# Attention over batches: the sum of two units in sixteen formed by TensorE with the identity, units handed on in the order 1, 2, 0, 3, product with v six steps behind

## What is computed

```python
# B = 8 batches, 32 heads of width d = 8, HW = 256 positions
xr = x.reshape(B, C, HW).transpose(0, 2, 1).reshape(B, HW, 32, d).transpose(0, 2, 1, 3)
q, k, v = split(einsum('brnd,ed->brne', xr, w_qkv) + b_qkv, 3)
attn = einsum('brnd,brmd->brnm', q, k)
attn = softmax(attn, axis=0)              # over the 8 batches, not over positions
out = einsum('brnm,brmd->brnd', attn, v)
```

## Time and profile before

| | |
|---|---|
| median of three runs | 654.94 us (652.09 to 654.96) |
| the profiled execution | 652.48 us |
| its span, first to last instruction | 650.7 us |
| TensorE busy (matmul / weight load) | 563.1 us (87%) / 359.0 us (55%) |
| VectorE busy | 476.3 us (73%) |
| ScalarE busy | 322.2 us (50%) |
| GpSimd busy | 385.1 us (59%) |
| mean granted TensorE clock | 0.926 of 2.4 GHz |

### The profile page before, as it was taken

The page is one execution under the profiler, slowest core; times in us unless marked ns, Lnnn a source line. Parts: engine busy times, 40 slices in busy tenths (PEclk is TensorE's granted clock), DMA queues, the critical chain, the costliest instruction groups (busy, mean ns, idle before and its releaser), DMA issues.

```text
span 650.7 us, 13039 instructions
## 1 busy us (share of the span) xinstructions
PE 563.1 (87%) x4540; PEld 359.0 (55%) x4541; DVE 476.3 (73%) x845; ACT 322.2 (50%) x687; POOL 385.1 (59%) x240
## 2 busy tenths in 40 slices
PE   3899667999999999999999996689973999999944
PEld 1555346655555555555555553679862565655633
DVE  5547865999999999999999995584866334333325
ACT  2533572677676767677676764232232333333310
POOL 2000371999999999999999997140005566666420
PEclk9998795899999999999999999699955999999985
DMA  6111066133233323333233200000032222222239
GB/s 207 55 47 33 2 224 257 74 105 115 85 90 104 100 85 89 101 101 95 81 97 103 58 1 3 1 1 1 2 122 46 71 87 90 83 82 90 65 106 323
DMA packets 34693, 56.58 MB, mean 87 GB/s; under 512 B 8693, under 2 KB 23438, under 8 KB 34382
## 3 DMA queue, kind: packets, MB, share of 16 engines
q1 hardware_dynamic: 30462, 45.26, 22.3%
q0 software_dynamic: 3744, 10.39, 5.2%
q10 hardware_dynamic: 432, 0.20, 0.1%
HBM read 38.43 MB, written 17.40 MB: 86 GB/s over the span
## 4 chain that ended last, share of the span: by engine, by line
POOL 40%; PE 36%; issue 9%; DVE 8%; DMA 2%; ACT 2%; SPq 1%; POOLq 1%; another core or an unknown queue 0%; DVEq 0%
POOL e_ring L371 39%; PE ps L1336 11%; PE ps L1352 5%; PE ps L1290 2%; PE ps L1092 2%; PE ps L1268 2%; PE ps L1281 2%; PE ps L1122 2%; PE ps L1081 2%; DVE stats L652 1%; PE ps L1228 1%; PE ps L1328 1%; PE ps L1344 1%; SPq L349 1%; PE ps L1068 1%
## 5 line engine op out<-in xcount | busy, mean ns | idle before, releaser
L371 POOL TENSOR_TENSOR e_ring<-e_ring,x_hat 128x1024 f32<-128x1024 f32 x128 | 272.7, 2134 | 35.8 <-ACT x_hat L545 23.6
L535 ACT ACTIVATE e_ring<-ps 128x1024 f32<-128x1024 f32 x128 | 131.1, 1024 | 94.8 <-PE ps L1175 94.8
L792 DVE TENSOR_REDUCE m_bf<-ps 128x128 bf16<-128x1024 f32 x128 | 157.0, 1227 | 10.4 <-PE ps L1166 10.4
L799 DVE TENSOR_REDUCE x_hat<-e_ring 128x128 f32<-128x1024 f32 x128 | 156.4, 1222 | 2.3 <-ACT e_ring L535 2.1
L1166 PE MATMUL ps<-q_stack,k_stack 72*128 72x128 bf16 x1024 | 139.0, 319 | 9.4 <-DMA k_stack<-qk_parts 9.4
L1166 PEld LDWEIGHTS ps<-q_stack,k_stack 72*128 72x128 bf16 x1024 | 103.9, 133 | 35.9 <-issue 35.9
L1175 PE MATMUL ps<-m_bf,ident_neg 128*128 128x512 bf16 x256 | 80.5, 397 | 13.4 <-DVE m_bf L792 5.8
L1189 PE MATMUL ps<-e_ring,v_slot 128*32 128x128 f32 x2048 | 85.4, 283 | 3.6 <-POOL e_ring L371 3.6
L1189 PEld LDWEIGHTS ps<-e_ring,v_slot 128*32 128x32 f32 x2048 | 49.8, 108 | 57.5 <-issue 52.6
L1336 PE MATMUL ps<-w_sb,e_ring 128*128 x156 | 75.4, 607 | 1.2 <-issue 1.2
L406 POOL DMA_INDIRECT pair_rows<-scratch,slot_y x39 | 38.5, 986 | 41.9 <-DVE scratch L1026 28.4
(11 more groups left out here) (150 smaller groups left out, 685.1 us busy)
## 6 DMA issues: line engine op xcount, KB each, us to landing
q_stack<-qk_parts SPq DMA_DIRECT2D x32, 288.0 KB
k_stack<-qk_parts SPq DMA_DIRECT2D x96, 96.0 KB
w_sb<-in_w13T_dram SPq DMA_DIRECT2D x16, 256.0 KB, 6.7
qk_parts<-scratch SPq DMA_DIRECT2D x2, 1536.0 KB, 19.1
qk_parts<-e_ring SPq DMA_DIRECT2D x2, 1152.0 KB, 5.5
x_res<-in_x_dram SPq DMA_DIRECT2D x8, 256.0 KB, 3.9
w_sb<-in_w2T_dram SPq DMA_DIRECT2D x8, 256.0 KB, 6.7
token_rows<-work SPq DMA_DIRECT2D x4, 512.0 KB, 3.0
```

The costliest lines, as they stand in the source:

```text
L371: nc.gpsimd.tensor_tensor(ev, ev, view(x_hat, CH + (u % RS) * P, [[0, BQ], [1, P], [0, 2]]), ALU.mult).then_inc(norm_done, 1)
L535: nc.scalar.activation(e_ring[:, u % ER, :], score_banks(v), ACT.Exp).then_inc(exp_done, 1)
L792: nc.vector.tensor_reduce(m_bf[:, u % 2], by_position(score_banks(v).rearrange("p a c -> p (a c)")), AXY, ALU.max).then_inc(max_done, 1)
L799: nc.vector.tensor_reduce(s_sum[:, u % 2], by_position(e_ring[:, u % ER, :]), AXY, ALU.add).then_inc(sum_done, 1)
```

## The change

The sums of units 0 and 8 of each group (`BY_PE`) are taken from VectorE. TensorE forms them with 8 matmuls each, the f32 identity as weights and the exponentials of one batch as the 128 columns, accumulated in 128 columns of PSUM bank 7. The eight matmuls are spread over three steps (`SUM_PARTS`: batches 0 to 2, 3 to 5, 6 and 7), two, three and four steps behind the unit's scores, between subtract and product. ScalarE's logarithm reads these two sums from bank 7.

Units are handed from the logarithm on in the order 1, 2, 0, 3, ... and 9, 10, 8, 11, ... (`ORDER`). Logarithm and inverse run three steps behind instead of two, the product six instead of five (`LAG`), and with it evacuate, transposes and add_heads move one step. `s_sum` becomes a ring of four, and `s_ln` moves to columns behind `s_inv`. New waits: the adds wait for the exponentials, for the logarithm of the sum that was in the bank before, and (unit 8) for add_heads; the transposes wait for the logarithm of unit 0.

```diff
-    LAG = 5
+    LAG = 6
+    ORDER = (1, 2, 0, 3, 4, 5, 6, 7, 9, 10, 8, 11, 12, 13, 14, 15)
+    BY_PE = (0, 8)
+    SUM_PARTS = ((0, 1, 2), (3, 4, 5), (6, 7))
+    RSUM = 4
...
             def weights(k, p):
                 pool.wait_ge(r_done, k + 1)
                 ev = e_ring[:, ORDER[p] % ER, :]
...
             def exponentials(U, v, u):
                 act.wait_ge(sub_done, U + 1)
                 if later_than(U, ER):
-                    act.wait_ge(pv_done, U - ER + 1)
+                    act.wait_ge(pv_done, position(U - ER) + 1)
...
+            def logarithm(k):
+                U = unit(k)
+                if U % UPG in BY_PE:
+                    act.wait_ge(pe_sums, sums_by_pe(U))
+                    total_of = ps[:, 7, 0:P]
+                else:
+                    act.wait_ge(sum_done, sums_by_dve(U))
+                    total_of = s_sum[:, U % RSUM]
+                nc.scalar.activation(s_ln[:, k % 2], total_of, ACT.Ln).then_inc(ln_done, 1)
...
-                if has(2):
-                    logarithm(U - 2, (u - 2) % UPG)
-                    inverse(U - 2, (u - 2) % UPG)
+                if has(3):
+                    logarithm(U - 3)
+                    inverse(U - 3)
...
-            def total(U, u):
+            def total(U):
                 dve.wait_ge(exp_done, U + 1)
-                if later_than(U, 2):
-                    dve.wait_ge(ln_done, U - 1)
+                if U >= RSUM and (U - RSUM) % UPG not in BY_PE:
+                    dve.wait_ge(ln_done, position(U - RSUM) + 1)
...
-                if has(1):
-                    total(U - 1, (u - 1) % UPG)
-                if u == LAG + 2 and has(LAG + 3):
+                if has(1) and (U - 1) % UPG not in BY_PE:
+                    total(U - 1)
+                if u == LAG + 3 and has(LAG + 4):
                     add_heads(g, g)
...
+            def add_batches(U, part):
+
+                batches = SUM_PARTS[part]
+                if part == 0:
+                    pe.wait_ge(exp_done, U + 1)
+                    if U % UPG == BY_PE[1] and U >= UPG:
+                        pe.wait_ge(x2_added, U // UPG)
+                    if U >= UPG // 2:
+                        pe.wait_ge(ln_done, position(U - UPG // 2) + 1)
+                for b in batches:
+                    last = nc.tensor.matmul(ps[:, 7, 0:P], ident[:], view(e_ring, (U % ER) * UW + (b // 2) * (2 * P) + b % 2, [[2, P]]),
+                                            start=(b == 0), stop=(b == B - 1), skip_group_check=True)
+                if part == len(SUM_PARTS) - 1:
+                    last.then_inc(pe_sums, 1)
...
                 if has(1):
                     subtract(U - 1, v - 1, (u - 1) % UPG)
+                for part in range(len(SUM_PARTS)):
+                    if has(2 + part) and (U - 2 - part) % UPG in BY_PE:
+                        add_batches(U - 2 - part, part)
                 if has(LAG):
-                    product(U - LAG, (u - LAG) % UPG, g)
+                    product(U - LAG, g)
                 if u == LAG + 1 and has(LAG + 2):
+                    pe.wait_ge(ln_done, position(g * UPG + BY_PE[0]) + 1)
                     transpose_heads(g)
```

More of the change, by code:

```diff
@@ L129, in conv_stack_kernel @@
                  for buf in (e_ring[:, 2:8, :].rearrange("p a b -> p (a b)"), scratch[:, :])]
-        s_sum = x_hat[:, 0, 0:2 * P].rearrange("p (s n) -> p s n", s=2)
-        s_ln = x_hat[:, 0, 2 * P:4 * P].rearrange("p (s n) -> p s n", s=2)
+        s_sum = x_hat[:, 0, 0:RSUM * P].rearrange("p (s n) -> p s n", s=RSUM)
+        s_ln = x_hat[:, 0, CH + RS * P:CH + (RS + 2) * P].rearrange("p (s n) -> p s n", s=2)
         s_inv = x_hat[:, 0, CH:CH + RS * P].rearrange("p (s n) -> p s n", s=RS)
@@ L206, in conv_stack_kernel @@
         stack_in = [sem(f"stack_in{i}") for i in range(HPG)]
+        pe_sums = sem("pe_sums")
         scores_done, max_done, sub_done, exp_done, sum_done, ln_done = (
@@ L248, in attention_steps, with unit, position, sums_by_pe @@
                 step(UNITS + u, UNITS + u, u, NG, lambda k: k > u)
+        def unit(k):
+            return k // UPG * UPG + ORDER[k % UPG]
+        def position(U):
+            return U // UPG * UPG + ORDER.index(U % UPG)
+        def sums_by_pe(U):
+            return U // UPG * len(BY_PE) + sum(b <= U % UPG for b in BY_PE)
+        def sums_by_dve(U):
+            return U + 1 - sums_by_pe(U)
         def score_banks(v):
@@ L366, in _, with weights @@
                                         parts[s // 2][:, s % 2, 1, c * CH:(c + 1) * CH], ALU.subtract).then_inc(part3, 1)
[L368 to L371, removed]
+            def weights(k, p):
+                pool.wait_ge(r_done, k + 1)
+                ev = e_ring[:, ORDER[p] % ER, :]
+                nc.gpsimd.tensor_tensor(ev, ev, view(x_hat, CH + (p % RS) * P, [[0, BQ], [1, P], [0, 2]]), ALU.mult
                                         ).then_inc(norm_done, 1)
             with pool.Fori(0, NG) as g:
-                for u in range(UPG):
-                    weights(g * UPG + u, u)
+                for p in range(UPG):
+                    weights(g * UPG + p, p)
             for b in range(B):
@@ L535, in exponentials, with inverse @@
                 nc.scalar.activation(e_ring[:, u % ER, :], score_banks(v), ACT.Exp).then_inc(exp_done, 1)
[L537 to L545, removed]
+            def logarithm(k):
[7 more added lines that the diff above has]
+                nc.scalar.activation(s_ln[:, k % 2], total_of, ACT.Ln).then_inc(ln_done, 1)
+            def inverse(k):
+                act.wait_ge(ln_done, k + 1)
+                if k >= RS:
+                    act.wait_ge(norm_done, k - RS + 1)
+                nc.scalar.activation(s_inv[:, k % RS], s_ln[:, k % 2], ACT.Exp, scale=-1.0).then_inc(r_done, 1)
             def evacuate(g):
@@ L793, in maximum @@
                                         ).then_inc(max_done, 1)
-            def total(U, u):
+            def total(U):
                 dve.wait_ge(exp_done, U + 1)
-                if later_than(U, 2):
-                    dve.wait_ge(ln_done, U - 1)
-                nc.vector.tensor_reduce(s_sum[:, u % 2], by_position(e_ring[:, u % ER, :]), AXY, ALU.add).then_inc(sum_done, 1)
+                if U >= RSUM and (U - RSUM) % UPG not in BY_PE:
+                    dve.wait_ge(ln_done, position(U - RSUM) + 1)
+                nc.vector.tensor_reduce(s_sum[:, U % RSUM], by_position(e_ring[:, U % ER, :]), AXY, ALU.add).then_inc(sum_done, 1)
             def add_heads(g, group):
@@ L1178, in subtract, with product @@
                 last.then_inc(sub_done, 1)
-            def product(U, u, g):
+            def add_batches(U, part):
[11 more added lines that the diff above has]
+                    last.then_inc(pe_sums, 1)
+            def product(k, g):
+                p, u = k % UPG, unit(k) % UPG
                 i, mh, nh = u // 4, (u // 2) % 2, u % 2
-                if u % 4 == 0:
-                    pe.wait_ge(v_slot_ready[i], g + 1 if u < UPG - LAG else g)
-                if u == 0 and later_than(U, 1):
+                if p % 4 == 0:
+                    pe.wait_ge(v_slot_ready[i], g + 1 if p < UPG - LAG else g)
+                if p == 0 and k >= 1:
                     pe.wait_ge(acc_out, g)
-                pe.wait_ge(norm_done, U + 1)
+                pe.wait_ge(norm_done, k + 1)
                 for b in range(B):
@@ L1191, in product @@
                                             view(e_ring, (u % ER) * UW + (b // 2) * (2 * P) + b % 2, [[2, P]]),
-                                            start=(u == 0 and b < 4), stop=(u == UPG - 1), skip_group_check=True)
+                                            start=(p == 0 and b < 4), stop=(p == UPG - 1), skip_group_check=True)
                 last.then_inc(pv_done, 1)
```

## The result

The changed kernel takes 663.37 us (median, 660.05 to 664.27); before, with the runs taken beside it, 653.71. The ratio is 1.014, 95% interval 1.0094 to 1.0186. The forecast was 662.7. The profiled execution took 663.47 us with a span of 661.7 us, 11.0 more than before by either.

The account below looks back on a forecast made before the run. VectorE set the pace before; afterwards TensorE's 36.05 us floor plus 1.3 of waits gives 37.35 a group. Groups 5.1, first group 1.8 and end 2.1 sum to +9.0 on 653.7: 662.7 us, range 643 to 671.

Parts of the forecast that it names:

- TensorE's price of the adds: Attention, TensorE: 0.2225 us per f32 identity matmul, 3.56 us a group for sixteen, raising TensorE's floor to 36.05 us.
- The step of 2.00: Attention, TensorE running late: scores, subtraction and product take 0.83 + 0.57 + 0.60 = 2.00 us a step.
- rival C: Attention: a late TensorE step takes 1.85 us, not 2.00; period 35.1, total 644.6 us; chance 0.13.
- VectorE's saving is lost: Attention, steps 2 to 4: TensorE never waits, VectorE idles, and the time taken off VectorE is spent as idleness.
- the walk: Start times followed through a group's 16 attention steps using links from the trace; returned 36.7 us before, 37.35 after.
- Rival A: Attention: the adds fit in and VectorE stays the bound; 18 us saved before losses, total 639.5 us; chance 0.08.
- Rival B: Attention: TensorE's floor without waits sets a 36.05 us period; total 652.3 us, hardly a change; chance 0.15.
- Rivals D and E: D: adds cost more, 0.32 us a matmul, over 675 us, chance 0.08; E: change doesn't do what it says, 0.02.
- Two of the signs given for being right: Attention: VectorE idle 2.5 to 3 us a group before maxima, released by scores; no subtraction wait in steps with adds.
- The period: Attention, one group of 16 units: 36.05 us TensorE floor plus 1.3 of waits, 37.35 us, 0.64 slower.
- The end: End of attention, last exponential to last product: 8.0 us instead of 5.92, so +2.1 us.
- The first group: Start of attention: TensorE at half clock until 117.3 us, first adds at twice the price, 1.8 us more.

Follow-up runs that it names:

- the handing on alone: The change without its adds (VectorE keeps all sixteen totals, later order of handing on stays) against the kernel before: 659.0 us against 655.28, ratio 1.0067.
- one unit: The change with only unit 8 summed by TensorE in f32, unit 0 back on VectorE, against the kernel before: 658.21 us, ratio 1.0085.

## Why the prediction was right, point by point

**TensorE's price of the adds** held: 0.2225 us a matmul was forecast; blocks of 3, 3, 2 made steps of 2.68 and 2.46 where 2.67 and 2.45 were written down, halving gave 0.22 and doubling 0.226 each. The step of 2.00 held in every late step (2.00 to 2.01), so rival C is out: from the first of eight scores to the subtraction it is 0.84 us, 0.105 each. The Trainium skill (TensorE: Matmul & The Clock Gate, Back-to-back issue gap) gives about 81 ns for pairs of load and matmul of 128 columns; these rows don't bear that out.

**VectorE's saving is lost** held in kind. In the first half of the group hardly any of the total's 1.13 us is used: steps 2 to 4 are as long with as without it, and up to step 10 the difference is 0.13. In the second half more is used than the walk had, because the addition of heads stands there. Rival A would have had 639.5 and is out. The Trainium skill (Perfetto Trace Analysis, Identifying the Most-Contended Engine) judges TensorE's room by the busy share of its weight loads, beside the share of peak FLOPs. The trace doesn't bear that share out here: it was 57% before, and yet the group had only 0.66 us of room left behind the adds, and the order of steps took more than that. Rival B (36.05, no waits) is out too: the group is 37.70. Rivals D and E did not occur.

Two of the signs given for being right did not show. VectorE's gaps are 2.1 us a group, not 2.5 to 3, and they lie ahead of the totals, released by exponentials, not ahead of the maxima: the maximum runs as soon as its scores are there, while the exponential that the next total needs stands behind a subtraction that is late in TensorE's queue. And the subtraction does wait in two steps with adds, 0.29 in step 2 and 0.18 in step 10; the walk itself had 0.26 in step 2 and a wait in step 10, so that sign did not agree with the walk.

**The period** was forecast at 37.35 and measured at 37.70: 0.99 a group instead of 0.64. The walked starts of the scores agree with the trace within 0.15 us up to step 10 (23.3 against 23.2); step 10 then takes 3.11 against 2.9. The term that was most too small is that step: its two waits are 0.35 together where I had 0.22, and from the adds, which had to wait, to the product it is 0.85 instead of 0.77. The other 0.14 are some 0.01 a step on TensorE.

**The end** held: +2.1 forecast, 8.00 - 5.92 = 2.08 measured, 2.07 with the handing on alone.

**The first group** is the step of the prediction that failed. I charged 1.8 us for adds at half clock. In the changed kernel just the first block of three ran so; the next rows of TensorE are at full clock.

```profile
108.31 1.37 PE L1217 MATMUL ps<-e_ring,ident 128*128 128x128 f32 x6
109.52 1.04 PE L1193 MATMUL ps<-q_stack,k_stack 72*128 72x128 bf16 x8
...
110.82 0.84 PE L1217 MATMUL ps<-e_ring,ident 128*128 128x128 f32 x6
```

I had taken the moment at which the clock came up, 117.3 us, as given by the kernel. In the run without adds it was also at about 109, with bf16 adds at about 115. The rows of the run without adds:

```profile
106.25 1.91 PE L1193 MATMUL ps<-q_stack,k_stack 72*128 72x128 bf16 x8
107.87 1.14 PE L1202 MATMUL ps<-m_bf,ident_neg 128*128 128x512 bf16 x2
108.81 1.16 PE L1193 MATMUL ps<-q_stack,k_stack 72*128 72x128 bf16 x8
```

Up to there TensorE had the same work, with the same distances, as in the kernel before, whose scores at 108.45 and 111.01 still took 1.91 and 1.92 us. So TensorE's work in this stage up to the rise doesn't decide when it comes, and the adds don't show as its cause. Each kernel has one profile, so how far the moment moves between executions of the same kernel isn't shown. Less the end and seven periods, attention is 39.36 us before, 38.4 with the handing on alone and 39.1 in the change: the first group's adds cost 0.6 to 0.7 us, less than the 0.99 of a later group, and the run without adds was 0.9 shorter than the kernel before, which I put down to the earlier clock.

The two misses offset each other: seven times 0.35 = 2.5 too little, 2.7 too much at the start (0.64 + 1.8 forecast, -0.3 measured), and attention came out 8.7 us longer where 9.0 was forecast. The close total is partly this luck. The medians differ by 9.7 us, of which attention's 8.7 is all that the profiles assign; the 2.3 us outside attention in the profiled execution stay open.

## What to carry to other kernels

In these kernels two engines near their limits that hand work to each other in order did not reach the larger of their two floors: the period exceeded that floor by 1.4 us (one unit), 1.6 (the change) and 0.9 (one add in place of eight) of some 36. Before moving work from the packed engine to the one with room, walk a period with starts taken from the trace, and ask for each freed slot whether the other engine can use it in that very step. A saving in a step where the partner has become late is idle time; the same plan at half the price per matmul was a gain.

## What was not expected of the hardware

The clock of TensorE at the start of attention came up at 109 us in the change and in the run without adds, about 115 with bf16 adds, and 117 before, with the same first matmuls of the stage at 101.5 to 102.4 us; granted clock 0.50 until then, 1.00 after. Over the twelve profiles the rise lay between 107.8 and 117.4 us. Why it differs is open.

The experts' stage ranged over 4.7 us between profiles with the same instructions. Part of that seems to go with the chip: the first four experiments, all on one chip, lie at 124.3 to 124.8 us, the next four, on another, at 120.1 to 122.5, the last two, on a third, at 122.8 and 122.9. The 2.4 us between profiles of the second chip are open.
